# A four-layer graph network in FP32: each engine's order written out for the end of the edge stage, with one more node chunk

## What is computed

```
msg = relu(x[src] + edge_attr)                 # 21250 x 512
agg = segment_sum(msg, dst, 1250)
h   = x + agg
h   = relu(h @ W1 + b1) @ W2 + b2              # 512 -> 512 -> 512
h   = x + h
h   = (h - mean(h)) * rsqrt(var(h) + 1e-5) * gamma + beta   # over the nodes
out = layernorm(x + h)
```

## Time and profile before

| | us |
|---|---|
| median of 3 runs | 599.36 |
| the three runs | 599.36, 599.69, 595.47 |
| the profiled execution, its own time | 599.38 |
| its span, first to last instruction | 597.7 |
| mean granted TensorE clock | 0.929 |

### The profile page before, as it was taken

One profiled execution on the slowest core, in us unless ns is written; L12 is line 12 of the kernel. 1 busy time (PEld: TensorE's weight loads), 2 busy tenths in 40 slices (PEclk: granted clock), 3 DMA queues, 4 the chain that ended last, 5 costly groups with the idle time before them and its releaser, 6 DMA issues.

```text
span 597.7 us, 7939 instructions
## 1 busy us (share of the span) xinstructions
PE 499.0 (83%) x2461; PEld 344.5 (58%) x2461; DVE 396.0 (66%) x894; ACT 251.7 (42%) x435; POOL 303.1 (51%) x328
## 2 busy tenths in 40 slices
PE   4999999999999997999993446676879777799875
PEld 2544459997899943899882001133435434365765
DVE  7999986768758868111563637555776577687475
ACT  7677741131485127211025424343434435445235
POOL 8999829210013015930003777777777777773000
PEclk9999999999999999799997577788989989799989
DMA  7900000000001200000766899999999999973004
GB/s 259 269 1 0 2 2 1 0 1 1 1 1 33 109 0 0 2 0 0 293 234 246 299 400 365 381 383 397 395 385 357 401 394 400 383 201 101 2 1 172
DMA packets 35604, 102.64 MB, mean 172 GB/s; under 512 B 6635, under 2 KB 7277, under 8 KB 35562
## 3 DMA queue, kind: packets, MB, share of 16 engines
q1 hardware_dynamic: 22150, 58.51, 26.5%
q0 software_dynamic: 13344, 43.53, 20.1%
q10 hardware_dynamic: 68, 0.09, 0.0%
HBM read 96.99 MB, written 5.12 MB: 171 GB/s over the span
## 4 chain that ended last, share of the span: by engine, by line
PE 44%; POOL 14%; DVE 14%; DMA 12%; issue 8%; ACT 5%; DVEq 2%; ACTq 0%; SPq 0%
PE ps L1200 19%; POOL xg L490 14%; DMA xg<-x_dram,srcT_i 12%; PE ps L1223 10%; DVE hot_code L815 4%; PE ps L1345 2%; PE ps L1252 2%; PE ps L1377 2%; PE ps L1366 2%; PE ps L1155 2%; ACT countsT L592 2%; DVE counts L826 2%; DVE ea L1020 1%; DVE stats L904 1%; PE ps L1177 1%
## 5 line engine op out<-in xcount | busy, mean ns | idle before, releaser
L490 POOL DMA_INDIRECT xg<-x_dram,srcT_i x168 | 172.0, 1024 | 114.7 <-DMA x_dram<-xn 63.8
L1345 PE MATMUL ps<-ea,hot_w 128*32 128x512 f32 x336 | 99.8, 735 | 65.7 <-ACT ea L657 65.5
L1020 DVE TENSOR_TENSOR ea<-ea,xg 128x512 f32<-128x512 f32 x168 | 108.9, 690 | 35.5 <-DMA xg<-x_dram,srcT_i 35.2
L657 ACT ACTIVATE ea<-ea 128x2048 f32<-128x2048 f32 x41 | 78.3, 1910 | 116.7 <-DVE ea L1020 116.7
L1345 PEld LDWEIGHTS ps<-ea,hot_w 128*32 128x32 f32 x336 | 18.1, 123 | 125.5 <-ACT ea L657 72.2
L426 POOL TENSOR_SCALAR hot_lo<-iota_n,src_loT 128x128 bf16<-128x128 f16 x105 | 66.3, 648 | 3.2 <-PE ps L1155 2.3
L1035 DVE TENSOR_TENSOR x3T<-x3T,ps 128x128 f32 x84 | 24.3, 289 | 45.4 <-issue 27.7
L815 DVE TENSOR_SCALAR hot_code<-iota_c,codeT 128x380 bf16<-128x380 f16 x168 | 49.8, 356 | 1.7 <-issue 0.8
L1200 PE MATMUL ps<-counts,xs_hi 128*128 x120 | 45.4, 379 | 3.9 <-POOL xs_lo L450 3.9
L1200 PE MATMUL ps<-counts,xs_lo 128*128 x120 | 44.3, 369 | 0.0
L1177 PE MATMUL ps<-w_s,xT 128*128 128x512 f32 (+1 forms) x80 | 40.8, 591 | 0.0
(11 more groups left out here) (180 smaller groups left out, 946.6 us busy)
## 6 DMA issues: line engine op xcount, KB each, us to landing
ea<-in_edge_attr_dram SPq DMA_DIRECT2D x41, 1024.0 KB, 9.7
w_s<-in_L_gnn_W_dram SPq DMA_DIRECT2D x5, 1024.0 KB, 8.8
xg<-x_dram,srcT_i POOLq DMA_INDIRECT x168, 7.5
xn<-in_x_dram SPq DMA_DIRECT2D x3, 768.0 KB, 8.8
x_dram<-xn SPq DMA_DIRECT2D x9, 256.0 KB
out_dram<-xn SPq DMA_DIRECT2D x9, 256.0 KB
w_s<-in_L_gnn_W_dram SPq DMA_DIRECT2D x2, 512.0 KB, 12.2
b_b<-in_L_gnn_b_dram SPq DMA_DIRECT2D x3, 256.0 KB, 10.3
```

The source lines that it names most:

```text
L490: pool.indirect_dma_start(out=xg[0:n, slot, r, :], out_offset=None, in_=x3_dram[:, :], in_offset=bass.IndirectOffsetOnAxis(ap=srcT_i[0:n, ...
L657: act.activation(ea[s][:, :, :], ea[s][:, :, :], ACT.Relu).then_inc(relu_done, 1)
L1020: dve.tensor_tensor(ea[s][0:n, r, :], ea[s][0:n, r, :], xg[0:n, slot, r, :], ALU.add).then_inc(add_done, 1)
L1345: ins = pe.matmul(ps[at_w:at_w + EW, 4 + g // 2 % 2, :], hot_w[:, g % RING, 2 * b + r, :], ea[g % RING][:, 2 * b + r, :], start=(r == 0), ...
```

## The change

One more node chunk: `GROUP_CUTS` gets a cut at group 40, so the last 134 nodes are done as 60 and 74 (chunks 6 and 7 of now 8). Chunk 6 has columns 120 to 180 of `h1`, beside chunk 5 (`H1_COL`), so it needs only chunk 4 gone (`H1_FREE`). The loops end at group 41, and from group 35 on each engine's order comes from tables and hand-written lines. After, in the same notation:

- PE: scatter 37, out(4, 0-1), turn 18, scatter 38, out(4, 2-3), pre(5, 0-1), scatter 39, pre(5, 2-3), turn 19, scatter 40, out(5, 0-1), pre(6, 0-3), scatter 41, out(5, 2), turn 20, out(5, 3), out(6, 0), pre(7, 0-3), out(6, 1-3), out(7, 0-3)
- ACT: relu 37, hidden(4, 2-3), copy of pair 18, relu 38, relu 39, hidden(5, 0-1), copy of pair 19, relu 40, hidden(5, 2-3), relu 41, hidden(6, 0-3), copy of pair 20, hidden(7, 0-3)
- DVE: rows 37, pair 17, add(3, 2-3), rows 38, add(4, 0-1), pair 18, rows 39, add(4, 2-3), rows 40, rows 41, pair 19, add(5, 0-1), add(5, 2), pair 20, add(5, 3), add(6, 0-3), add(7, 0-3)

The node rows of tiles 2 and 3 of the last group (one row each) are fetched by two direct DMAs of SP, whose row numbers SP reads into registers, and no longer by POOL; DVE adds these two tiles first.

```
@@ -57,13 +57,19 @@
 FLAG_AT = 33
 ACT_LOS = (2, 1, 2, 1)
 NPAIR = NG // 2
-LATE = 9
 TURN_X = (18, 23)
-GROUP_CUTS = (8, 16, 22, 28, 34, 38, NG)
+GROUP_CUTS = (8, 16, 22, 28, 34, 38, 40, NG)
 GNODES, SLACK = 30, 24
 NODE_CUTS = [0] + [GNODES * g - SLACK for g in GROUP_CUTS[:-1]] + [N]
 NCUT = len(NODE_CUTS) - 1
 SOON = 16
+TURN_SOON = 18
+PRE_AT = ((11, 12), (19, 20), (25, 26), (31, 32), (35, 36), (38, 39), (40, 40))
+HIDDEN_AT = ((12, 13), (20, 21), (26, 27), (32, 33), (36, 37), (39, 40))
+OUT_AT = ((14, 16), (22, 24), (28, 30), (34, 36), (37, 38))
+ADD_AT = ((16, 18), (24, 26), (30, 32), (36, 37), (38, 39), (41, None))
+H1_COL = [0] * 6 + [NODE_CUTS[6] - NODE_CUTS[5], 0]
+H1_FREE = [0, 1, 2, 3, 4, 5, 5, 6]
 CMAX = max(b - a for a, b in zip(NODE_CUTS, NODE_CUTS[1:]))
 XTILES = 4
 TLAG = 3
@@ -71,7 +77,7 @@
 LN_SETS = ((0, 2), (2, 4), (4, 6), (6, 8), (8, 9), (9, 10))
 PE_SUMS = (2, 3, 5, 6, 8, 9)
 EPS = 1e-5
-assert CS * (NCH - 1) + CH == N and NCODE <= 512 and NG == 2 + NT * HOTS and NG % 2 == 0 and NB * EW * 2 == P and not any(g % 2 for g in GROUP_CUTS)
+assert LAST_P == 1 and LAST_R == 0 and CS * (NCH - 1) + CH == N and NCODE <= 512 and NG == 2 + NT * HOTS and NG % 2 == 0 and NB * EW * 2 == P and not any(g % 2 for g in GROUP_CUTS)
 assert BLOCK_SPAN * GE + 1 <= 4096 and BE < LAST < GE and (TPG * 2 + 3) * NG <= 512
 
 
@@ -279,6 +285,7 @@
         ea_loaded = [sem(f"ea_loaded{i}") for i in range(RING)]
         xg_loaded = [[sem(f"xg_loaded{i}_{r}") for r in range(TPG)] for i in range(XRING)]
         idx_seen = sem("idx_seen")
+        end_loaded = [sem(f"end_loaded{i}") for i in range(2)]
         add_done, relu_done, win_ready = sem("add_done"), sem("relu_done"), sem("win_ready")
         scat_done, zn_ready, turn_done, win_added = sem("scat_done"), sem("zn_ready"), sem("turn_done"), sem("win_added")
         fix_x, fix_e, fix_msg, fix_done, fix_added = (sem("fix_x"), sem("fix_e"), sem("fix_msg"), sem("fix_done"), sem("fix_added"))
@@ -310,9 +317,9 @@
 
             return edge_attr[g * GE:(g + 1) * GE, :].rearrange("(b p r) d -> p b (r d)", b=NB, r=2)
 
-        def at_chunk(q):
-
-            return GROUP_CUTS[q] + (1 if NCUT - 3 <= q < NCUT - 1 else 3)
+        def pieces(steps, g):
+
+            return [(q, 2 * i + c) for q, at_step in enumerate(steps) for i in range(2) if at_step[i] == g for c in range(2)]
 
         def pair_at(m):
 
@@ -394,6 +401,12 @@
             for g in range(early, NG):
                 load(g)
 
+            ends = [sp.value_load(srcT_i[0:1, r, NG - 1:NG], min_val=0, max_val=N - 1) for r in (2, 3)]
+            sp.wait_ge(x3_stored, 16 * NT)
+            for r, end in zip((2, 3), ends):
+                sp.wait_ge(add_done, TPG * (NG - 1 - XRING) + r + 1)
+                sp.dma_start(xg[0:1, (NG - 1) % XRING, r, :], x3_dram[bass.ds(end, 1), :]).then_inc(end_loaded[r - 2], 16)
+
             for j in range(NT):
                 sp.wait_ge(x_ready, 3 * NT + j + 1)
                 sp.dma_start(out[j * P:j * P + rows(j), :], xn[0:rows(j), j, :]).then_inc(out_stored, 16)
@@ -483,12 +496,11 @@
 
             def gather(g):
                 slot = g % XRING
-                for r in range(TPG):
+                for r in range(TPG if g < NG - 1 else 2):
                     if g >= XRING:
                         pool.wait_ge(add_done, TPG * (g - XRING) + r + 1)
-                    n = max(tile_rows(g, r), 2)
-                    pool.indirect_dma_start(out=xg[0:n, slot, r, :], out_offset=None, in_=x3_dram[:, :],
-                                            in_offset=bass.IndirectOffsetOnAxis(ap=srcT_i[0:n, r, g:g + 1], axis=0)).then_inc(xg_loaded[slot][r], 16)
+                    pool.indirect_dma_start(out=xg[:, slot, r, :], out_offset=None, in_=x3_dram[:, :],
+                                            in_offset=bass.IndirectOffsetOnAxis(ap=srcT_i[:, r, g:g + 1], axis=0)).then_inc(xg_loaded[slot][r], 16)
 
             for g in range(NG):
                 gather(g)
@@ -671,18 +683,24 @@
                 n = NODE_CUTS[q + 1] - NODE_CUTS[q]
                 act.wait_ge(pre_done, q * KC + f + 1)
                 if q and f == 0:
-                    act.wait_ge(h2_done, q * KC)
-                act.activation(h1[:, f, 0:n], ps[:, 2 + f % 2, 0:n], ACT.Relu, bias=cols[:, 1, f:f + 1]).then_inc(h1_ready, 1)
-
-            for g in range(NG + LATE):
-                if g < NG:
-                    rectify(g)
-                if g % 2 == 0 and 2 <= g <= NG:
+                    act.wait_ge(h2_done, H1_FREE[q] * KC)
+                act.activation(h1[:, f, H1_COL[q]:H1_COL[q] + n], ps[:, 2 + f % 2, 0:n], ACT.Relu, bias=cols[:, 1, f:f + 1]).then_inc(h1_ready, 1)
+
+            for g in range(NG):
+                rectify(g)
+                if g % 2 == 0 and 2 <= g < 2 * TURN_SOON + 2:
                     evac_pair(g // 2 - 1)
-                for q in range(NCUT):
-                    if g in (at_chunk(q) + 1, at_chunk(q) + 2):
-                        for f in halves(g - at_chunk(q) - 1):
-                            hidden_chunk(q, f)
+                for q, f in pieces(HIDDEN_AT, g):
+                    hidden_chunk(q, f)
+                    if g == 2 * TURN_SOON + 1 and f == KC - 1:
+                        evac_pair(TURN_SOON)
+                if g == 2 * TURN_SOON + 3:
+                    evac_pair(TURN_SOON + 1)
+            for f in range(KC):
+                hidden_chunk(NCUT - 2, f)
+            evac_pair(NPAIR - 1)
+            for f in range(KC):
+                hidden_chunk(NCUT - 1, f)
 
             act.wait_ge(bn_step, 2 * KC)
             act.activation(bn_t[:, 0, :], bn_mv[:, :, 1:2].rearrange("p c a -> p (c a)"), ACT.Sqrt, bias=eps_s[:, 0:1]).then_inc(bn_sq, 1)
@@ -1014,8 +1032,11 @@
 
                 s, slot = g % RING, g % XRING
                 dve.wait_ge(ea_loaded[s], 16 * (g // RING + 1) + 16 * (g == NG - 1))
-                for r in range(TPG):
-                    dve.wait_ge(xg_loaded[slot][r], 16 * (g // XRING + 1))
+                for r in range(TPG) if g < NG - 1 else (2, 3, 0, 1):
+                    if g == NG - 1 and r >= 2:
+                        dve.wait_ge(end_loaded[r - 2], 16)
+                    else:
+                        dve.wait_ge(xg_loaded[slot][r], 16 * (g // XRING + 1))
                     n = tile_rows(g, r)
                     dve.tensor_tensor(ea[s][0:n, r, :], ea[s][0:n, r, :], xg[0:n, slot, r, :], ALU.add).then_inc(add_done, 1)
                 if g >= RING:
@@ -1047,17 +1068,22 @@
                 if q == NCUT - 1:
                     ins.then_inc(bn_step, 1)
 
-            for g in range(NG + LATE):
-                if g < NG:
-                    add_rows(g)
-                for m in range(NPAIR):
+            for g in range(NG):
+                add_rows(g)
+                for m in range(TURN_SOON):
                     if g == pair_at(m):
                         add_pair(m)
-                for q in range(NCUT - 1):
-                    if g in (at_chunk(q) + 5, at_chunk(q) + 7):
-                        for cc in halves((g - at_chunk(q) - 5) // 2):
-                            add_chunk(q, cc)
-
+                if g == NG - 1:
+                    add_pair(NPAIR - 2)
+                for q, cc in pieces(ADD_AT, g):
+                    add_chunk(q, cc)
+                if g == 2 * TURN_SOON + 2:
+                    add_pair(TURN_SOON)
+            add_chunk(NCUT - 3, 2)
+            add_pair(NPAIR - 1)
+            add_chunk(NCUT - 3, 3)
+            for cc in range(KC):
+                add_chunk(NCUT - 2, cc)
             for cc in range(KC):
                 add_chunk(NCUT - 1, cc)
                 dve.wait_ge(bn_step, 2 * cc + 1)
@@ -1374,22 +1400,33 @@
                 if q * KC + cc >= 2:
                     pe.wait_ge(h2_ready, q * KC + cc - 1)
                 for k in range(KC):
-                    ins = pe.matmul(ps[:, cc % 2, 0:n], w32_s[:, k, P * cc:P * cc + P], h1[:, k, 0:n],
+                    ins = pe.matmul(ps[:, cc % 2, 0:n], w32_s[:, k, P * cc:P * cc + P], h1[:, k, H1_COL[q]:H1_COL[q] + n],
                                     start=(k == 0), stop=(k == KC - 1))
                 ins.then_inc(h2_done, 1)
 
-            for g in range(NG + LATE):
-                if g < NG:
-                    scatter(g)
-                if g % 2 == 0 and 2 <= g <= NG:
+            for g in range(NG):
+                if g in (2 * TURN_SOON + 2, 2 * TURN_SOON + 4):
                     turn(g // 2 - 1)
-                for q in range(NCUT):
-                    if g in (at_chunk(q), at_chunk(q) + 1):
-                        for f in halves(g - at_chunk(q)):
-                            pre_chunk(q, f)
-                    if g in (at_chunk(q) + 3, at_chunk(q) + 5):
-                        for cc in halves((g - at_chunk(q) - 3) // 2):
-                            out_chunk(q, cc)
+                scatter(g)
+                if g % 2 == 0 and 2 <= g < 2 * TURN_SOON + 2:
+                    turn(g // 2 - 1)
```

(17 more changed lines are left out.)

## The result

| | before | after |
|---|---|---|
| median | 599.08 us (6 runs, 595.47 to 599.87) | 616.77 us (6 runs, 614.74 to 618.03) |
| span of the profiled execution | 597.7 | 616.3 |
| mean granted TensorE clock | 0.929 | 0.913 |

Ratio 1.0297, 95% interval 1.0270 to 1.0324: the change makes the kernel 17.7 us slower. I had forecast 607.9 (602 to 611). The direction was right, the size half of it.

The account below looks back on a forecast made before the run. PE's own work was taken to bound the end of the edge stage. Work 6.9, holes 2.3 and tail -0.3 gave 8.9, step by step 8.5; 599.4 + 8.5 = 607.9 us, range 602 to 611.

Parts of the forecast that it names:

- what bounds the kernel: End of the edge stage: PE's own work queue; 3.1 us of holes can be filled, 6.9 us of work goes in.
- the price of a narrow piece: Chunks 6 and 7 on PE: 0.111 us a pass at either width, set by the weight load; 0.89 us a piece.
- B: Chunks 6 and 7: narrow passes cost only their columns, no added work, holes get filled; 596.3 us, chance 0.05.
- C: Chunks 6 and 7: passes cost only their columns, but the new order's holes come; 602.7 us, chance 0.06.
- The added work: PE, chunks 6 and 7: 16 pieces in 14.2 us against 7.3 for eight before, 6.9 us more.
- the two holes: PE idle 2.6 us before scatter 39 and 2.4 before pre(7), through DVE's late register reads of pairs 18 and 20.
- rival A: DVE runs its register reads ahead of the waiting `bn_stats`, so only PE's added work counts; 603.2 us, chance 0.16.
- SP's row loads and POOL's lighter list: Last group's gathers: priced at nothing, as nobody waits for them; below 1 us if the cover went.
- parts 1 and 2: End of the edge stage: the extra chunk adds 6.9 us of PE work; the new order's holes are 5.4 against 3.1.
- rival D: PE's clock falls in a new hole; one such stretch costs 1.7 to 3.5 us; 610.5 us, chance 0.13.

Follow-up runs that it names:

- e12_reads: Changed kernel with DVE reading the registers of pairs 18 and 20 one step earlier, run a second time; 602.45 us against 599.05, ratio 1.0063.
- e1_pad: Changed kernel, same order, with chunks 6 and 7 streaming 106 to 134 columns a pass, extra results unread; 659.36 us against 650.12, ratio 1.0139.
- e2_reads: Changed kernel with DVE reading the registers of pairs 18 and 20 one step earlier, first run; 650.90 us against 650.12, ratio 1.0039.
- e3_nocut: Changed kernel's new order without the extra chunk, the last 134 nodes again one chunk; 650.63 us against 650.12, ratio 0.9997.
- e6_reads20: Changed kernel with only pair 20's register reads one step earlier; 654.96 us against 654.54, ratio 1.0094.
- e4_split: Kernel before with only the extra chunk added, 60 and 74 nodes in the old order; 667.60 us against 650.12, ratio 1.0287.
- e7_split_pad: Kernel before with the extra chunk in the old order, its passes streaming 120 and 134 columns; 656.15 us against 654.54, ratio 1.0117.
- e5_after: Changed kernel run once more with nothing altered, as a control; 662.41 us against 654.54, ratio 1.0230.
- e9_fill: Changed kernel with six unread 128x512 matmuls added on PE right ahead of pre(7); 655.97 us against 650.28, ratio 1.0143.

## Why the prediction was half right

**Right: what bounds the kernel.** PE's own list bounds the end of the stage. e12_reads is the purest case: full clock, no holes over 0.5 us, one chunk more. I had said that even with no hole at all the end would come 3.7 us later; its stretch is 4.0 longer, its total 3.4.

**Right: the price of a narrow piece.** 0.110 us a pass at 60 columns. Rivals B and C, which priced by the columns (0.051), are out. The added work is 6.9 us by my price. The rule on weight loads of the Trainium skill (TensorE: Matmul & The Clock Gate, "LDWEIGHTS (loading the stationary operand)"), 107 ns for 128 columns, agrees with the 0.110 us measured here at full clock to 3%.

**Right: the two holes, in place, length and cause.** 2.31 and 2.52 us against 2.6 and 2.4. The forecast start times agree less well than they look: pre(7) starts 33.1 us behind scatter 37 where the first hole doesn't take the clock (e1_pad), 34.5 in the kernel after and 32.8 in the forecast, and the stretch began 1.0 us early. e2_reads takes both away by moving two groups of register reads, so the cause is shown and rival A is out.

**Right, though only argued: SP's row loads and POOL's lighter list.** The fetches of SP were issued at 537.9, sixteen microseconds ahead of their use, and nobody in the trace waits for them. No run undid this part alone.

**Wrong: the clock.** The step that failed is the price of the clock. Every term of parts 1 and 2 silently takes it at 1.00, and rival D, in which it falls, says: "One such stretch in the end costs 1.7 to 3.5 us". I took the price of one low stretch from around 520 us, where PE did 512-column work right after. I didn't ask what PE would be doing behind the new hole. It was doing 88 passes of 60 and 74 columns. The same passes take 18.5 us from start to end after (572.80 to 591.34) and 10.05 in e12_reads (563.38 to 573.43), so 8.5 us; scatter 39 and pre(5, 2-3) lost 0.8 each behind the first hole (2.70 for 1.91, 2.88 for 2.04), some 1.5 of it in the end. In all some 10 us in the stretch, against 0 in my forecast and 3.5 at most in D. Whether the 0.7 behind the stretch is the clock too is not shown. D's lower price, 1.7, is about right where wide work follows the hole (1.5 to 1.7 behind the first one, 1.8 in e3_nocut and 5.59 - 3.83 = 1.8 again in e1_pad); what it lacked is the case of narrow work behind it.

**The balance of the 18.9 us in the stretch:** one more chunk, holes filled as far as they go, 4.0 (e12_reads against before); the two holes, 4.9 (2.4, e6_reads20 against e12_reads, and 2.5); the clock, the remaining 10.0, of which the 1.5 behind the first hole don't come in every execution. I had forecast the first two (8.5 together) and missed the third, which also was what made the range of 602 to 611 too narrow: two of my own terms, the narrow passes and the holes, make each other dearer, and I had only added them.

Rows 3 held the hint: a scatter at 3.57 us shows that this clock does fall after a hole of a microsecond or two in this kernel. With D's chance at 0.13 for one stretch, I had not asked how long a stretch could last.

## What to carry to other kernels

A chunk cut narrower than its weight load makes no pass cheaper: a pass with a 128x128 FP32 load took 0.110 us at 60 columns and 0.111 at 120. Worse, in the three profiles where the clock fell with such passes behind, they didn't bring it back, so a gap of 2.5 us in front of them cost 8.5 us more than itself; keep narrow work away from gaps, or stream it wider, or put wide matmuls into the gap. And when a pair of operations starts with register reads, put the reads ahead of the last instruction that waits: an engine's list stops at a wait, and the 2.7 us of reads come on top if they stand behind it.

## What the runs showed of the hardware that I had not expected

- **Useless columns made a kernel faster.** 60 more columns in each of 128 passes, with the same gaps, took the stretch from 52.3 to 42.8 us (e4_split, e7_split_pad); 5.2 us of matmuls that nobody reads saved 6.6 us behind them (e5_after, e9_fill).
- **At the lower clock a load-bound pass doubles almost exactly**, 0.213 against 0.110 us, and a single load takes 333 ns against 190: the load follows the clock too.
- **A busy PE in the profile is no sign of a full clock.** From 580 to 592 us after, PE is busy for 11.35 of 12 us and the granted clock is 0.50; one has to read the clock's own column. The Trainium skill, TensorE: Matmul & The Clock Gate, section "What's actually happening", says that activity releases the throttle. This trace doesn't bear that out for PE's busy time: busy for 18 us on end, the clock stayed at 0.50.
- **Chips differ in the edge stage**: the kernel before took 599 us on one chip of the experiments and 650 to 655 on two others, and there only a stretch of the trace, not the total, could tell 5 us.
